# Second attention on one TensorE core: scores from stacked hi/lo operands, one unrolled pipeline, operands laid out through device memory

## The reference, cut to what matters

```python
q = x_q @ w_q                       # 16 heads of 16 features
kv = x_kv @ w_kv                    # keys and values of the raw context, 77 rows
logits = jnp.einsum('bhqd,bhkd->bhqk', q, k) * SCALE     # SCALE = 16 ** -0.5
rel = arange(Tq)[:, None] - arange(Tk)[None, :]
logits = logits + (rel[..., None] * w_rel[0]).transpose(2, 0, 1)[None]
attn = jax.nn.softmax(logits, axis=-1)
out = jnp.einsum('bhqk,bhkd->bhqd', attn, v)
x = x + out.transpose(0, 2, 1, 3).reshape(B, Tq, 256) @ w_proj     # x_q is layernorm(x)
```

## Time and profile before

| Measure | Value |
|---|---|
| Device time, median of three | 1285.13 us |
| Profiled execution, first to last instruction (span) | 1284.3 us |
| TensorE busy | 1155.0 us (90%) |
| VectorE busy | 946.6 us (74%) |
| ScalarE busy | 744.9 us (58%) |
| GpSimd busy | 443.5 us (35%) |
| Mean granted TensorE clock | 0.944 of full speed |

### The profile page before, as it was taken

How to read it: one execution, slowest core, us unless ns; L and a number is a source line. 1 busy time by engine, 2 the same in 40 slices (tenths; PEclk the granted TensorE clock), 3 DMA queues, 4 the chain that set the end, 5 groups by cost and what they waited for, 6 DMA issues and landing times. The chain is left out here.

```text
span 1284.3 us, 31779 instructions
## 1 busy us (share of the span) xinstructions
PE 1155.0 (90%) x9045; PEld 1104.0 (86%) x9045; DVE 946.6 (74%) x2439; ACT 744.9 (58%) x2297; POOL 443.5 (35%) x656
## 2 busy tenths in 40 slices
PE   7689999999999987999996799999999947767998
PEld 7689999999999987999996699999999837767777
DVE  3567777677776666777776688888888659997656
ACT  3466677567765654333332577677677516666754
POOL 0232222322322210221213454554555346664015
PEclk9889999999999998999998799999999968999559
DMA  7010000000000001000000000000000000000103
GB/s 239 23 67 1 0 0 0 0 0 0 0 0 0 0 2 29 1 0 0 0 0 4 2 1 0 0 0 0 0 0 0 1 18 1 1 0 1 39 27 123
DMA packets 20583, 18.63 MB, mean 15 GB/s; under 512 B 6620, under 2 KB 19644, under 8 KB 20412
## 3 DMA queue, kind: packets, MB, share of 16 engines
q1 hardware_dynamic: 19724, 17.45, 4.3%
q10 hardware_dynamic: 816, 0.66, 0.2%
HBM read 13.89 MB, written 4.19 MB: 14 GB/s over the span
## 5 line engine op out<-in xcount | busy, mean ns | idle before, releaser
L770 POOL TENSOR_TENSOR att_prob<-att_ex,att_rinv 128x308 f32<-128x308 f32 x256 | 179.8, 705 | 326.1 <-DVE att_rinv L651 290.6
L610 ACT ACTIVATE att_ex<-att_s_bank,att_mx 128x77 f32<-128x77 f32 x1024 | 250.2, 334 | 17.1 <-DVE att_mx L641 15.2
L674 DVE TENSOR_TENSOR att_pT_lo<-att_t_bank,att_pT_hi 128x512 fp32r<-128x512 f32 x256 | 176.6, 690 | 50.4 <-ACT att_pT_hi L588 48.1
L486 PE MATMUL att_s_bank<-att_keys,att_qT 128*128 128x154 f32 x1024 | 205.5, 315 | 0.0
L588 ACT CAST att_pT_hi<-att_t_bank 128x512 fp32r<-128x512 f32 x256 | 150.0, 587 | 75.2 <-PE att_t_bank L496 70.3
L510 PE MATMUL att_o_bank<-att_pT_hi,att_vals_hi 128*128 128x256 f32 x512 | 167.5, 327 | 5.1 <-DVE att_pT_lo L674 2.9
L486 PEld LDWEIGHTS att_s_bank<-att_keys,att_qT 128*128 128x128 f32 x1024 | 152.7, 194 | 6.7
L496 PE MATMUL att_t_bank<-all_ident,att_prob 128*128 128x128 f32 x1024 | 152.9, 272 | 0.0
L510 PE MATMUL att_o_bank<-att_pT_lo,att_vals_hi 128*128 128x256 f32 x512 | 144.1, 281 | 0.0
L510 PE MATMUL att_o_bank<-att_pT_hi,att_vals_lo 128*128 128x256 f32 x512 | 143.9, 281 | 0.0
L618 ACT ACTIVATE att_qT<-att_q_bank 128x256 f32<-128x256 f32 x160 | 61.6, 385 | 136.9 <-PE att_q_bank L462 135.9
(11 more groups left out here) (215 smaller groups left out, 3363.0 us busy)
## 6 DMA issues: line engine op xcount, KB each, us to landing
all_x<-in_x SPq DMA_DIRECT2D x4, 1024.0 KB, 8.1
out<-comb_y SPq DMA_DIRECT2D x16, 256.0 KB, 2.1
all_raw<-in_L_ffn_w SPq DMA_DIRECT2D x2, 1024.0 KB, 5.8
moe_w_raw<-in_L_ffn_w SPq DMA_DIRECT2D x32, 64.0 KB, 2.1
pro_ctx_in<-in_ctx SPq DMA_DIRECT2D x4, 308.0 KB
all_raw<-in_L_xattn_W_q SPq DMA_DIRECT2D x1, 1024.0 KB, 8.2
all_raw<-in_L_xattn_W_o SPq DMA_DIRECT2D x1, 1024.0 KB, 10.7
pro_w_raw<-in_L_xattn_w_kv ACTq DMA_DIRECT2D x1, 512.0 KB, 4.8
```

The lines of the kernel that those rows point to most:

```text
L486: last = nc.tensor.matmul(out, qT[c % 2][:, q * P:(q + 1) * P], keys[:, kc, h0:h0 + 2, :], start=first, stop=True)
L610: last = nc.scalar.activation(ex[t % RING][:, r, :], s_bank[t % 2][:, r * SK:(r + 1) * SK], ACT.Exp, bias=mx[t % 2][:, r:r + 1])
L674: nc.vector.tensor_tensor(pT[t % 2][1][:, :], t_bank[t % 2][:, :], fp32_of(pT[t % 2][0][:, :]), ALU.subtract).then_inc(pt_lo, 1)
L770: nc.gpsimd.tensor_tensor(out, e, w, ALU.mult).then_inc(p_ready, 1)
```

## The change

`attention` becomes two functions. `attention0` is the first attention as it was, with added transfers; `attention1` is new.

- Prologue: the keys of the second attention are scaled by 16 ** -0.5 through their weights and, like its values, kept as a high and a low part. That adds a ScalarE copy and a VectorE subtraction per group of keys and per sequence of values.
- `attention0`: SyncE writes the layouts for the second attention to device memory: 4 transfers of 64 rows and 16 of 13 rows for the values, 16 of zeros (96 rows of 4928 bytes), then 48 of 16x16 pieces of 77 keys. Then the weights of `ffn` are loaded, as before.
- `attention1`: for each sequence the queries are split in a high and a low part and moved on chip by 12 transfers of 32 rows into `qs`, 96 rows that hold high, low and high parts, above four rows of positions; the keys `ks` stand opposite as high, high and low, above the bias. One fp32r product of 100 rows for each half then makes the scores of two heads, in place of a bf16 and an fp32 product.
- The first 64 of the 77 keys of two heads share one 128-wide transpose, and the last 13 of all heads (`tails`) are transposed as a unit of their own: five units of four transposes and six value products a sequence in place of eight.
- The sequences run in one written-out pipeline of stages with three sequences in flight; projection and residual of a sequence lie two stages behind its scores.

The diff, cut to its core:

```diff
+                    nc.scalar.mul(out, w_raw[:, :, lo:hi], DK1 ** -0.5).then_inc(w_hi, 1)
...
+                    dve.wait_ge(val1_hi, g * G + k + 1)
+                    nc.vector.tensor_tensor(st.val1[1][0:SK, bass.ds(g * G + k, 1), :],
+                                            val_ps[k % 2][0:SK, DK0:VC].unsqueeze(1),
+                                            fp32_of(st.val1[0][0:SK, bass.ds(g * G + k, 1), :]), ALU.subtract).then_inc(val_done, 1)
...
+            def spill_values():
+                count = 0
+                for part in range(2):
+                    v = fp32_of(st.val1[part][:, :, :])
+                    for h in range(2):
+                        sp.dma_start(st.vd_dram[:, MAIN * h:MAIN * h + MAIN, part, :].rearrange("b k e -> k b e"),
+                                     v[0:MAIN, :, :]).then_inc(spilled, 16)
...
+                    for h in range(8):
+                        sp.dma_start(st.vt_dram[:, TAIL * h:TAIL * h + TAIL, part, :].rearrange("b k e -> k b e"),
+                                     v[MAIN:SK, :, :]).then_inc(spilled, 16)
...
+                for b in range(B):
+                    sp.dma_start(st.ks_dram[b].rearrange("p c r h k -> p (c r h k)"), zeros[0:96, :]).then_inc(zeros_out, 16)
...
+                for k, part in enumerate((0, 0, 1)):
+                    for r in range(4):
+                        for h in range(2):
+                            a, at = 32 * r + DK1 * h, 32 * k + DK1 * h
+                            for c in range(DC):
+                                sp.dma_start(st.ks_dram[:, at:at + DK1, c, r, h, :].rearrange("b p k -> p b k"),
+                                             fp32_of(st.key1[part][a:a + DK1, c, :, :])).then_inc(spilled, 16)
...
+            spills = spill_values() + spill_keys()
+            sp.wait_ge(spilled, 16 * spills)
+            sp.wait_ge(w_ready, 2)
+            load_raw(sp, d, st, ("L0_ffn_w1", "L0_ffn_w2"), raw_in)
+            sp.wait_ge(raw_in, 32)
...
+            pool.memset(zeros[:, :], 0.0).then_inc(zero_ready, 1)
...
+        UNIT_AT = {0: 0, 1: 1, 3: 2, 4: 3, 6: 4}
+        CHUNKS = {0: (0, 1), 1: (2, 3), 2: (4, 5), 4: (6, 7)}
+        TAIL_UNIT = 3
...
+            def load_queries(f):
+                i = f % 2
+                sp.wait_ge(q_lo, f + 1)
+                at_least(sp, s_psum, HP * (f - 1))
+                for k, part in enumerate((0, 1, 0)):
+                    for r in range(4):
+                        sp.dma_start(fp32_of(qs[i][32 * k:32 * k + 32, :, :]).rearrange("p (c r) n -> p c r n", c=DC)[:, :, r, :],
+                                     fp32_of(qT[part][32 * r:32 * r + 32, :, :])).then_inc(qs_in[i], 16)
+            def load_keys(f):
+                i = f % 2
+                at_least(sp, s_psum, HP * (f - 1))
+                sp.dma_start(fp32_of(ks[i][0:BIAS, :, :, :, :]).rearrange("p c r h k -> p (c r h k)"),
+                             st.ks_dram[f].rearrange("p c r h k -> p (c r h k)")).then_inc(ks_in[i], 16)
+            def load_values(f):
+                i = f % 2
+                at_least(sp, vals_ready, VALS * (f - 1))
+                sp.dma_start(vd[i][:, :, :], st.vd_dram[f]).then_inc(v_in[i], 16)
...
+            for f in range(B):
+                load_queries(f)
+                if 1 <= f < B - 1:
+                    load_keys(f + 1)
+                    load_values(f + 1)
...
+            def scores(f, t):
+                i = f % 2
+                if t == 0:
+                    pe.wait_ge(qs_in[i], 16 * QS_DMAS * (f // 2 + 1))
+                    pe.wait_ge(ks_in[i], 16 * KS_DMAS * (f // 2 + 1))
+                if t == 0 and f < 2:
+                    pe.wait_ge(bias_in, 128)
+                    pe.wait_ge(pos_ready, 2)
+                at_least(pe, ex_ready, HP * f + t - 1)
+                for q in range(NC):
+                    last = nc.tensor.matmul(s_bank[t % 2][:, q * PAIR:(q + 1) * PAIR], qs[i][0:ROWS, t, q * P:(q + 1) * P],
+                                            ks[i][0:ROWS, t // 4, t % 4, :, :], start=True, stop=True)
+                last.then_inc(s_psum, 1)
...
+            for f in STAGES:
+                for t in range(HP):
+                    if here(f):
+                        scores(f, t)
+                    if here(f - 1) and t in UNIT_AT:
+                        transpose_p(f - 1, UNIT_AT[t])
+                    if t == 0 and here(f - 2):
+                        weigh_values(f - 2, 4)
+                    if t == 0 and here(f + 1):
+                        transpose_x(f + 1)
+                    if t == 1 and here(f + 1):
+                        queries(f + 1)
+                    if here(f - 1) and t in (2, 3, 5, 6):
+                        weigh_values(f - 1, {2: 0, 3: 1, 5: 2, 6: 3}[t])
+                    if t == 4 and here(f - 2):
+                        project(f - 2)
...
+                for i in range(2):
+                    nc.vector.tensor_copy(qs[i][BIAS:ROWS, :, :], pos_raw[BIAS:ROWS, :].unsqueeze(1).to_broadcast([4, HP, N])).then_inc(pos_ready, 1)
...
+            for f in STAGES:
+                for t in range(HP):
+                    if here(f):
+                        find_maxima(f, t)
+                    n = HP * f + t - 2
+                    if 0 <= n < HP * B:
+                        add_up(n // HP, n % HP)
+                    if t == 1 and here(f - 2):
+                        split_heads(f - 2, 1)
+                    if t == 2 and here(f + 1):
+                        split_queries(f + 1)
+                    if 0 <= n < HP * B:
+                        invert(n // HP, n % HP)
+                    if here(f - 1) and t in UNIT_AT:
+                        split_probs(f - 1, UNIT_AT[t])
+                    if t == 0 and here(f + 1):
+                        transposed_x(f + 1)
+                    if t == 7 and here(f - 1):
+                        split_heads(f - 1, 0)
+                    if t == 5 and here(f - 2):
+                        add_residual(f - 2)
+                    if t == 5 and here(f + 2):
+                        ln.statistics(dve, f + 2)
+                    if t == 7 and here(f + 2):
+                        ln.normalise(dve, f + 2, xt_psum, 1)
...
+            def weigh(f, t):
+                n = HP * f + t
+                pool.wait_ge(inv_ready, n + 1)
+                if f > 0 and t % 2 == 0:
+                    pool.wait_ge(t_psum, UNITS * (f - 1) + unit_of(t) + 1)
+                e = ex[t % RING][:, :, :].rearrange("p (q h) k -> p q h k", q=NC)
+                w = rinv[t % RING][:, :].rearrange("p (q h) -> p q h", q=NC).unsqueeze(3)
+                main = prob[:, :, t * P:(t + 1) * P].rearrange("p q (h k) -> p q h k", h=2)
+                tail = tails[f % 2][:, :, t * 2 * TAIL:(t + 1) * 2 * TAIL].rearrange("p q (h k) -> p q h k", h=2)
+                nc.gpsimd.tensor_tensor(main, e[:, :, :, 0:MAIN], w.to_broadcast([P, NC, 2, MAIN]), ALU.mult).then_inc(p_ready, 1)
...
+                nc.gpsimd.tensor_tensor(tail, e[:, :, :, MAIN:SK], w.to_broadcast([P, NC, 2, TAIL]), ALU.mult).then_inc(p_ready, 1)
...
+            ln.inverse_deviation(pool, 0)
+            for i in range(2):
+                for part in range(2):
+                    pool.memset(fp32_of(vmain[i][part][:, :]), 0.0).then_inc(vmain_zero, 1)
+            for f in STAGES:
+                for t in range(HP):
+                    n = HP * f + t - 2
+                    if 0 <= n < HP * B:
+                        weigh(n // HP, n % HP)
+                    if t == 5 and here(f + 2) and f + 2 > 0:
+                        ln.inverse_deviation(pool, f + 2)
+                    if t == 3 and here(f):
+                        lay_out_values(f)
...```

What moves on TensorE. In a step of the second attention before, with `t_bank` the transposed probabilities, `s_bank` the scores and `o_bank` the weighed values (of six passes and two halves, one turn is shown):

```order
L496 MATMUL att_t_bank<-all_ident,att_prob 128x128 x4
L484 MATMUL att_s_bank<-att_bias,att_pos 128x154
L486 MATMUL att_s_bank<-att_keys,att_qT 128x154
L510 MATMUL att_o_bank<-att_pT_hi,att_vals_hi 128x256
L510 MATMUL att_o_bank<-att_pT_lo,att_vals_hi 128x256
L510 MATMUL att_o_bank<-att_pT_hi,att_vals_lo 128x256
```

More of the change, by code:

```diff
@@ L477, in scores @@
                     first = True
-                    if L0 and q == 0:
+                    if q == 0:
                         nc.tensor.matmul(out, ident16[:, :], causal16[:, :], start=True, stop=False)
-                        first = False
-                    if not L0:
-                        nc.tensor.matmul(out, pos16[:, q * P:(q + 1) * P], bias16[:, 2 * t:2 * t + 2, :], start=True, stop=False)
                         first = False
@@ L566, in _ @@
             pe.wait_ge(c_ready, 1)
-            if not L0:
-                pe.wait_ge(bias_in, 96)
             loop(pe, batch)
```

433 lines of the change are left out of this document (341 added, 92 removed).

## The result

| Kernel | Median, us (fastest, slowest) | Runs |
|---|---|---|
| before | 1284.34 (1283.14, 1287.58) | 4 |
| changed | 1275.26 (1274.60, 1278.84) | 4 |

The ratio is 0.9934, 95% interval 0.9914 to 0.9953: faster, but by 9 us where 43 were forecast. The span went from 1284.3 to 1272.6 us. The time is 11 us above the top of the range.

What follows compares the result with a forecast made beforehand. TensorE bounded the second attention before, VectorE after. Start +14, first stage -3, 15 stages -51, end -5 and prologue +2.5 made -42.5: 1241.8 us, 1243 as a median, shaded to 1241; eight in ten between 1224 and 1264.

Steps and rivals of the forecast that it cites:

- VectorE as the next bound, 15.1 at least, 15.5 taken: Second attention: VectorE's work sets a stage's floor at 15.1 us, at most 16.2; 15.5 taken, against 18.9 before.
- The restack, hidden with 1.3 us to spare: The 12 on-chip query transfers of a stage take 8.0 us, at most 9.7, and hide behind other work.
- The cover of 9.3: VectorE's work from the end of the query split to its next stage, 9.3 us, which would hide the restack.
- Waits above the floor, 0.3 us: Query passes on TensorE, ahead of step 2's scores, wait for VectorE's split of x: nothing, or 0.3 us.
- TensorE 12.1 a stage: TensorE's work in a stage of the second attention after the change: 12.1 us, between 9.9 and 15.0.
- Start: Second attention's first score at 727, 14 us later than 713.1, with normalising possibly held up 4.4 us by memsets.
- Stage 0, 14 us: The second attention's first stage, bound by the next restack: 14 us where before it took 16.8, 3 less.
- End: Five probability units and the projection take about 13 us, where eight units took 18.4: 5 less.
- Spill: Writing the layouts to device memory takes 60 to 200 us, hidden by the first attention: zero in the sum.
- The shading of 2 us to 1241: Forecast lowered from 1243 to 1241 because start and stage were both taken from the upper half of their bounds.
- the longer ring: Rival, chance 0.17: a ring of waits sets a second-attention stage at 16.3 to 17.5 us, giving 1263.
- The falling clock: Rival, chance 0.05: TensorE's granted clock falls through the whole second attention, some 22 us a stage, giving 1340.

Runs made afterwards that it cites:

- e10: e9 with the statistics of x in step 3 instead of 5, inverse deviation in step 4 and normalising in step 6 instead of 7: 1233.26 us.
- e13: e10 with the restack by way of the device scratch, as in e12: 1231.67 us.
- e4: The changed kernel with 28 more 256-column matmuls on TensorE ahead of each stage's first scores: 1260.94 us.
- e3: The changed kernel with the transposes of the next x, and VectorE's split of it, ahead of a stage's first scores: 1251.74 us.
- e9: The changed kernel with the edits of e3, e6 and e7 together: 1242.84 us.
- e6: The changed kernel with GpSimd's four memsets of the value tiles held back until VectorE's first normalising is done: 1271.93 us.
- e7: The changed kernel with the 8 transfers of the rounded queries issued once rounded, the remainder's 4 last: 1260.21 us.
- e1: The changed kernel with 8 instead of 12 transfers in each restack after the second (output differs): 1250.19 us.
- e12: The changed kernel with queries restacked through a device scratch, two writes then six reads, the rounded ones going first: 1243.45 us.
- e2: The changed kernel with four more transfers of 64 bytes in each restack, to a tile nothing reads: 1316.51 us.
- e11: e10 with 12 more 256-column matmuls a stage, two at the end of each of six steps: 1230.31 us.
- e14: e13 with the 12 added matmuls a stage of e11: 1230.51 us.

## Why the prediction was wrong

- **VectorE as the next bound, 15.1 at least, 15.5 taken:** right as a floor, reached by e10 and e13 (15.4 and 15.5), not by the changed kernel. VectorE's busy time in it is 82.3 of 100 us, or 14.7 of a stage of 17.9.
- **The restack, hidden with 1.3 us to spare: the step that failed.** It had three parts. Its length was taken as 8.0, by 0.49 an issue; it is 9.4 on the mean of 14, by 0.64, near the end of 9.7 that I had and discounted: 1.4. Of the two rows, 0.49 was a load from device memory and 0.63 a move on chip, as the restack is; I went by the size where the kind of transfer was the likeness. The cover of 9.3 was counted on VectorE's list as if the part ahead of it, 15.5 - 9.3 = 6.2 us from first scores to the end of the query split, ran at VectorE's pace. That part is a chain over four engines and takes 8.5: 2.3 more. And the two together are a ring, for the next restack can't start before the scores of this one: 9.4 + 8.5 = 17.9. From the forecast's 8.0 + 6.2 = 14.2 the ring grew by 3.7, of which 1.3 were spare and 2.4 show.
- **Why the chain is longer:** the low clock after each wait makes 1.6 us of it (e4); the transposes of x stand behind work for the sequence before (e3 takes them out). I asked what a late restack would delay, but not what the lateness does to the next restack.
- **Waits above the floor, 0.3 us:** too small. The normalising in step 7 feeds the transposes of step 0, and this is 0.8 us a stage (e9 to e10). It was not in the sum.
- **TensorE 12.1 a stage:** 73.0 of 100 us busy, 13.1 a stage, a part of it at half speed; with the clock at 1.00 it is 12.2 (e13). Narrow products: two in 0.18 us from start to start (769.31 to 769.49), so 0.09 each, below the 0.135 that I took. GpSimd about 9.9 where I had 11 to 15; its 256-wide product takes 618 ns against 702 for 308 columns, and the second, 52 wide, 281.
- **Start:** first score expected at 727 plus a prologue of 2.5, 729.5; it came at 729.51. That it fits so well is luck: the transposes of x came at 713.51 where these sums give 715.2, 1.7 early, and from there the queries took 6.8 for 6.3 and the restack 9.2 for 8.0. The normalising did wait for the memsets, 4.85 us against 0.73 in e6, as the 4.4 of the prediction had it. The Trainium skill (GPSIMD Engine Reference, Key points) says that GpSimd shares its on-chip memory interfaces with VectorE and contends with its two-port modes. That the two contend, the trace agrees, by the 4.85 and 0.73 above; in which mode VectorE ran, no row shows.
- **Stage 0, 14 us:** 16.9 (729.51 to 746.38), the same ring. **End:** from the last maxima at 1007.56 to the end of the last sum into x at 1022.21, 14.6, forecast 13.4. **Spill:** hidden; `ffn` starts at 490.71, 2.7 later than the earlier trace rows, all of it from the prologue.
- **The sum:** 15 stages, 746.38 to the last maxima at 1007.56, took 261.2 for 232.5: +28.7. With stage 0 +2.9, the end +1.2 and the rest -1.6 this is 31.2, against a miss of 30.8 in the span. The shading of 2 us to 1241 went the wrong way: it held the stage of 15.5 for the upper half of the bounds, and the stage came out 2.4 above it.
- **The rivals:** the longer ring "(scores, maxima, exponentials, restack) at 16.3 to 17.5", at 0.17, came nearest, priced 12 us too low and half right. The restack is in the ring, but maxima and exponentials are not: behind the scores it runs through the transposes of x, its queries and their splits (e3, e7), and without the restack's issues the stage falls (e1). What spoke for it, 15 transfers from one queue, stood in the text. The test that I named, first scores waiting for `att_qs`, showed it at once. The falling clock, at 0.05, is there in part: half speed behind each wait, a mean of 0.85 to 0.87, not through the whole phase, and worth 14 us (e4).

## What to carry to other kernels

When a change puts a transfer between two engines, write out the whole round, from the landing through every engine to the next issue, and compare its length with the stage. A sum over the busiest engine's list is a floor, not a cover. Where many transfers are small (here 64 KB and less), count them by number, not bytes, and on the queue that issues them; price an issue by a row of the same kind of move. Then look for what can leave the round (work that doesn't need the transfer goes ahead of the wait: 23.5 us in e3), as well as for a shorter transfer (17 us in e12 against e7). Each alone ends at the next limit, so look for that one too.

## What was not expected of the hardware

- Issuing a move on chip takes 0.62 to 0.64 us on SyncE whether it carries 64 bytes (e2) or 64 KB; writes of 256 KB from 128 rows take 0.34 (e12). On ScalarE four took 2.83.
- TensorE that idles 4 us in every stage comes back at half clock (granted 0.50): four transposes 0.71 and six value passes 1.43, against 0.44 and 0.81 before. 28 added matmuls in the idle time avoid it, but for one stage, and are worth 14 us while the ring bounds (e4); 12 a stage are worth 3 or less when it doesn't (e11, e14).
- GpSimd's product of 52 elements costs 281 ns, that of 256 elements 618.
